# Hiding the scores that a count has found: a pass of VectorE, or four subtractions of GpSimd

## What is computed

```python
dots = einsum('bhid,bhjd->bhij', q, k) * scale          # j: 16 memory keys, then 512
dots = einsum('bhij,hk->bkij', dots, pre_proj)
dots = where(causal, -max, dots)
vk = lax.top_k(dots, 64)[0][..., -1:]                    # the 64th largest of each row
dots = where(dots < vk, -max, dots)
attn = softmax(dots)
attn = einsum('bhij,hk->bkij', attn, post_proj)
out = einsum('bhij,bhjd->bhid', attn, v) ... @ Wo + bo
```

## Time and profile before

| | |
|---|---|
| median of 3 runs | 3666.67 us |
| the profiled execution | 3667.18 us |
| its span, first to last instruction | 3665.3 us |
| granted TensorE clock, mean | 0.878 |
| busy: DVE, ACT | 3356.8 us (92%), 3202.9 us (87%) |
| busy: PE, PEld, POOL | 2800.9, 1814.3, 1432.8 us (76%, 49%, 39%) |
| DVE by line | L1017 522.2, L983 516.1, L1030 502.5, L1064 443.4, L1052 396.1 us |
| POOL by line | L1236 546.1, L1243 338.5 us |

### The profile page before, as it was taken

The page is one execution under the profiler, slowest core; times in us unless marked ns, Lnnn a source line. Parts: engine busy times, 40 slices in busy tenths (PEclk is TensorE's granted clock), DMA queues, the critical chain, the costliest instruction groups (busy, mean ns, idle before and its releaser), DMA issues. The chain is left out here.

```text
span 3665.3 us, 67866 instructions
## 1 busy us (share of the span) xinstructions
PE 2800.9 (76%) x13751; PEld 1814.3 (49%) x13751; DVE 3356.8 (92%) x13778; ACT 3202.9 (87%) x9018; POOL 1432.8 (39%) x2407
## 2 busy tenths in 40 slices
PE   7777878777767877777777767777777787777755
PEld 3455555555544555555455545554455455445544
DVE  4699999999999999999999999999999999999994
ACT  1799999999978999999999979998999999999973
POOL 3233443343334443444443334343444344343433
PEclk9888898889888989889899888989889889898986
DMA  1000000000000000000000000000000000000000
GB/s 41 7 2 2 4 8 5 8 2 5 8 4 8 5 8 2 5 8 5 8 5 8 2 4 8 5 8 2 5 8 5 8 2 6 6 5 8 2 7 4
DMA packets 31377, 22.38 MB, mean 6 GB/s; under 512 B 3202, under 2 KB 30339, under 8 KB 30723
## 3 DMA queue, kind: packets, MB, share of 16 engines
q1 hardware_dynamic: 30722, 16.03, 1.5%
HBM read 11.83 MB, written 4.19 MB: 4 GB/s over the span
## 5 line engine op out<-in xcount | busy, mean ns | idle before, releaser
L840 ACT ACTIVATE signs<-scores,state 128x528 int8<-128x528 f32 (+3 forms) x3072 | 1764.3, 574 | 200.4 <-DVE state L1122 124.0
L1236 POOL TENSOR_SCALAR probs<-probs,rinv 128x528 f32<-128x528 f32 (+3 forms) x1024 | 546.1, 552 | 1696.0 <-DVE rinv L1022 1694.8
L682 PE MATMUL s_bank<-xn,gT 128*128 128x512 f32 (+3 forms) x2048 | 916.3, 576 | 2.3 <-issue 1.5
L706 PE MATMUL t_bank<-ident,probs 128*128 128x128 f32 x2560 | 477.8, 311 | 283.5 <-POOL probs L1236 275.5
L693 PEld LDWEIGHTS y_bank<-u_all,probsT 128*128 128x128 f32 x5120 | 620.5, 195 | 134.0 <-issue 124.9
L693 PE MATMUL y_bank<-u_all,probsT 128*128 128x128 f32 x5120 | 625.3, 278 | 6.9 <-ACT probsT L851 6.8
L840 ACT ACTIVATION_READ_ACCUMULATOR signs<-scores,state 128x1 f32 x3072 | 576.0, 187 | 0.0
L1017 DVE SCALAR_TENSOR_TENSOR probs<-scores,kth,expo 128x528 f32<-128x528 f32 (+3 forms) x1024 | 522.2, 565 | 31.1 <-issue 23.6
L706 PEld LDWEIGHTS t_bank<-ident,probs 128*128 128x128 f32 x2560 | 299.1, 153 | 485.9 <-issue 380.6
L861 ACT ACTIVATE expo<-scores,negmax 128x528 f32<-128x528 f32 (+3 forms) x1024 | 535.1, 575 | 0.0
L983 DVE TENSOR_SCALAR_CACHE_REDUCE work<-scores,state 128x528 f32<-128x528 f32 (+3 forms) x1024 | 516.1, 559 | 17.8 <-issue 8.1
(11 more groups left out here) (152 smaller groups left out, 3577.7 us busy)
## 6 DMA issues: line engine op xcount, KB each, us to landing
xwork<-in_L_attn_x_dram SPq DMA_DIRECT2D x17, 256.0 KB, 2.8
xres<-in_L_attn_x_dram SPq DMA_DIRECT2D x16, 256.0 KB, 2.9
out_dram<-ybuf SPq DMA_DIRECT2D x16, 256.0 KB, 2.4
u_all<-in_L_attn_Wq_dram SPq DMA_DIRECT2D x1, 512.0 KB, 3.8
u_all<-in_L_attn_Wk_dram SPq DMA_DIRECT2D x1, 512.0 KB, 4.6
u_all<-in_L_attn_Wv_dram SPq DMA_DIRECT2D x1, 512.0 KB, 5.4
u_all<-in_L_attn_Wo_dram SPq DMA_DIRECT2D x1, 512.0 KB
expo<-in_L_ffn_w_gate_dram SPq DMA_DIRECT2D x1, 192.0 KB, 4.8
```

Of the source, the lines that this page charges most:

```text
L682: nc.tensor.matmul(score_part(t, 0, KEYS[t]), lhsT=gT[s % 2][:, t * P:(t + 1) * P], rhs=xn[par][:, 0:KEYS[t]], start=True, stop=False, ski ...
L706: mm = nc.tensor.transpose(t_bank[q % 2][:, at:at + P], probs[:, h % 2, KEY_AT[t] + j * P:KEY_AT[t] + (j + 1) * P], ident[:, :])
L840: nc.scalar.activation(signs[:, k, 0:ROW[t]], row(scores, ring(head_of(s, k + 1), RING), t), ACT.Sign, bias=state[:, s % 2, S_T, k * T + t ...
L1236: nc.gpsimd.tensor_scalar(prb, prb, rinv[:, slot_p, t:t + 1], 1.0, ALU.mult, ALU.mult).then_inc(scaled, 1)
```

## The change

L1052 goes. In its place POOL subtracts `work` from the scores, tile by tile, each as soon as DVE's count of that tile is done. So that subtracting 1 is enough to push a found score below all others, scores are kept in units of 2^60: the factor on the products that they are made of is 2^-60 smaller, the guesses, the mask and the maxima follow, and the exponential multiplies by 2^60. The counts of DVE now raise a semaphore of their own, `found_ready`, and POOL answers with `hidden`, on which MAX8 waits. On POOL the copy of the memory scores moves ahead of the subtractions, and these stand ahead of the scaling.

```diff
-MASKED = -2.0 ** 100
+UNIT = 2.0 ** -60
+MASKED = -2.0 ** 40
...
-            table[i, t] = z
-            table[i, T + t] = z - FAR / (2 * density)
+            table[i, t] = z * UNIT ** 0.5
+            table[i, T + t] = (z - FAR / (2 * density)) * UNIT ** 0.5
...
-                              DH ** -0.5).then_inc(a_taken, 1)
+                              DH ** -0.5 * UNIT).then_inc(a_taken, 1)
...
                                                  bias=negmax[:, bass.ds(ring(head_of(s, LAG_K), RING), 1), t]
+                                                 scale=1.0 / UNIT
...
 def count_found(t):
     v.tensor_scalar(work[:, AT[t]:AT[t] + ROW[t]], row(scores, slot_k, t), guessed[:, t:t + 1],
-                    None, ALU.is_ge, ALU.add, accum_out=found[:, t:t + 1]).then_inc(select_step, 1)
+                    None, ALU.is_ge, ALU.add, accum_out=found[:, t:t + 1]).then_inc(found_ready, 1)
...
-                        v.scalar_tensor_tensor(out=work[:, :], in0=work[:, :], scalar=-FMAX,
-                                               in1=scores[:, bass.ds(slot_k, 1), :].squeeze(1),
-                                               op0=ALU.mult, op1=ALU.add).then_inc(select_step, 1)
-                        dve.wait_ge(select_step, T + 2)
+                        dve.wait_ge(select_step, 2)
...
 def top_scan():
     if selects:
-        dve.wait_ge(select_step, T + 4)
+        dve.wait_ge(hidden, 4 * gk + 4)
+        alone(dve)
         for t in ORDER:
             v.max(cand[:, t, 1:9], work[:, AT[t]:AT[t] + ROW[t]]).then_inc(select_step, 1)
...
+                    if lagged(kind, s, LAG_K):
+                        slot_k = ring(head_of(s, LAG_K), RING)
+                        for p, t in enumerate(ORDER):
+                            pool.wait_ge(found_ready, 4 * (g - LAG_K) + p + 1)
+                            alone(pool)
+                            wrk = work[:, AT[t]:AT[t] + ROW[t]]
+                            nc.gpsimd.tensor_tensor(wrk, row(scores, slot_k, t), wrk, ALU.subtract).then_inc(hidden, 1)
```

More of the change, by code:

```diff
@@ L416, in build @@
         counted = [sem(f"counted{k}") for k in range(GUESSES)]
+        found_ready = sem("found_ready")
+        hidden = sem("hidden")
         select_step = sem("select_step")
@@ L935, in _ @@
             dve.wait_ge(a_taken, 4)
-            nc.vector.tensor_tensor(a_sq[:, :, :], a_all[:, :, :], a_all[:, :, :], ALU.mult).then_inc(squared, 1)
+            nc.vector.scalar_tensor_tensor(out=a_sq[:, :, :], in0=a_all[:, :, :], scalar=1.0 / UNIT, in1=a_all[:, :, :],
+                                           op0=ALU.mult, op1=ALU.mult).then_inc(squared, 1)
             dve.wait_ge(squared, 1)
@@ L1228, in step @@
                                               seed[:, s, :, :]).then_inc(first_ready, 1)
+                    if kind != "drain":
+                        if s == 0:
+                            pool.wait_ge(memmax_ready, b + 1)
+                        slot = ring(head_of(s, 0), RING)
+                        if kind != "first" or s >= RING:
+                            pool.wait_ge(probs_ready, 4 * (g - RING + 1))
+                        alone(pool)
+                        nc.gpsimd.tensor_copy(mem_parts(scores[:, bass.ds(slot, 1), :].squeeze(1)),
+                                              head_mem(smem[par], s)).then_inc(mem_placed, 1)
+                    if lagged(kind, s, LAG_K):
+                        slot_k = ring(head_of(s, LAG_K), RING)
+                        for p, t in enumerate(ORDER):
+                            pool.wait_ge(found_ready, 4 * (g - LAG_K) + p + 1)
+                            alone(pool)
+                            wrk = work[:, AT[t]:AT[t] + ROW[t]]
+                            nc.gpsimd.tensor_tensor(wrk, row(scores, slot_k, t), wrk, ALU.subtract).then_inc(hidden, 1)
                     if lagged(kind, s, LAG_P):
@@ L1243, in step @@
                         nc.gpsimd.tensor_copy(head_mem(pmem, head_of(s, LAG_P)), mem_parts(probs[:, slot_p, :])).then_inc(pmem_ready, 1)
-                    if kind != "drain":
-                        if s == 0:
-                            pool.wait_ge(memmax_ready, b + 1)
-                        slot = ring(head_of(s, 0), RING)
-                        if kind != "first" or s >= RING:
-                            pool.wait_ge(probs_ready, 4 * (g - RING + 1))
-                        alone(pool)
-                        nc.gpsimd.tensor_copy(mem_parts(scores[:, bass.ds(slot, 1), :].squeeze(1)),
-                                              head_mem(smem[par], s)).then_inc(mem_placed, 1)
                     extras(kind, b, s)
```

16 lines of the change are left out of this document (8 added, 8 removed).

## The result

The changed kernel takes 3679.9 us (median of 6 runs, 3677.9 to 3684.9) against 3667.0 us of the kernel before on the same chip: ratio 1.0037, 95% interval 1.0026 to 1.0049. It is slower, by 13 us. The forecast said slower, but by 38 us; its range, 3620 to 3850, holds the time. The profiled execution, the slowest of its six, has a span of 3683.1 us against 3665.3, 17.8 more. Its mean granted TensorE clock is 0.877 against 0.878, so the clocks are alike.

What follows compares the result with a forecast made beforehand. DVE was taken to bound the kernel, ACT close behind. Step growths of 1.05 + 0.58 + 0.15 + 0.15 + 0.45 = 2.38 us a batch made +38 us in 16 batches: 3667 + 38 = 3705 us, range 3620 to 3850.

Steps and rivals of the forecast that it cites:

- Which engine bounds: DVE, 92% busy, sets the time; ACT stands only tenths of a us behind in steps without norm or feed-forward.
- The turns: DVE instructions with two SBUF inputs, or DVE copies, alternate whole with POOL instructions reading SBUF; here masking pass and subtractions.
- the forecast order: After POOL's first subtraction, masking of 528 elements goes first, then the subtraction of 400, alternating down to 144.
- Forecast delay of the chain: Masking pass ends 1.60 us later, or 1.46 in most steps, where it already starts 0.14 later; bounds 0 and 2.67.
- the forecast's rule: The waiting engine's instruction ends 0.02 us plus its elements' time behind the other's, on DVE and on POOL.
- DVE keeps its turn: Rival: the four masking instructions run back to back, later small ones are stopped 1.3 us against 1.31 saved; 3665 us, chance 0.20.
- They do not meet: Rival: masking pass and two-input POOL instructions do not exclude each other, so 1.31 us stay saved; 3463 us, chance 0.12.
- No start-up hides: Rival: the three later subtractions cost DVE their whole time, delay 2.67 us, +1.36 a step; 4015 us, chance 0.08.
- Not the same work: Rival: counts or power on POOL fail at 1e-18, guesses miss and the full search runs; +2700 us, chance 0.02.
- The step that failed: POOL's memory-keys copy moves ahead of the subtractions, beside one-input MAX8; no cost or gain was counted for it.
- 1.31 us: Time saved per DVE step by removing L1052: 1.35 us, less 0.04 for the wait and nop ahead of MAX8.
- growth forecast: Growth by step kind: seven +0.15, two +0.29, three with f_up and three with norm +0.05, one +0.45; batch +2.38 us.

Runs made afterwards that it cites:

- the run with the fill: Changed kernel with each POOL subtraction replaced by a memset of the same tile to -1, which reads nothing: 3486.0 us, ratio 0.950.
- one input: Changed kernel with each POOL subtraction replaced by a one-input multiplication of the same tile by -1 and 1: 3484.3 us, ratio 0.950.
- the run of four elements: Changed kernel with each POOL subtraction covering only 4 elements and MAX8 reading the scores themselves: 3483.3 us, ratio 0.950.
- the run of the units alone: Changed kernel with the subtraction back on DVE as one instruction; 2^60 units, semaphores, wait and nop, and earlier memory copy stay: 3659.6 us, ratio 0.9981.
- the copy put back: Changed kernel with POOL's memory-keys copy back behind L1263, as in the kernel before; DVE's program unchanged: 3700.6 us, ratio 1.0085.
- a changed order: Changed kernel with DVE taking new scores from PSUM ahead of the masking pass, and MAX8 ahead of the small block and guess chain: 3504.3 us, ratio 0.956.

## Why the prediction was right in its mechanism and wrong in its size

**Which engine bounds.** Right. DVE sets the changed kernel; ACT waits more for turned tiles (L854 waits 210.8 us for PE, where L851 waited 109.8), and that costs DVE next to nothing, as worked out (its own wait for the counts is 20.8 us against 19.3).

**The turns.** Right. Forecast: L1022 of about 0.9, 1.4, 1.0 and 0.6 us; measured, in the 193 heads of the forecast order, 0.77 to 0.85, 1.40, 0.99 and 0.58. The forecast did not see the other order, of 51 heads; that the mean of the first, 0.94, is also close to 0.9 is luck. Forecast delay of the chain 1.46 us in steps where it starts at +2.07, and 1.60 where it starts at +1.93; measured, as medians over the batches, 1.48 and 1.57. The rule of a turn (the waiting one ends its elements plus a small constant behind the other, its start-up being over) was read from two rows, and in the 244 heads of both orders every turn ended within 0.07 us of the forecast's rule. The constant is about 0.01 us for DVE behind POOL and 0.05 for POOL behind DVE, where 0.02 was taken for both. POOL's was too small because the forecast's 1.06 ns an element compared a copy of 64 elements with a scaling of 528. The scaling's own four sizes in the run with the fill (708, 602, 499 and 390 ns) give 0.83. At that, an estimate for a copy, the one that ended 0.09 us behind L1052 had 0.05 for its elements and 0.04 besides. The Trainium skill, SBUF — State Buffer, "Who interferes with whom", says that a two-input DVE instruction contends with a GpSimd instruction that reads SBUF and not with one that only writes. The runs with one input and with the fill agree, each with its rows above. The rule of the Trainium skill against this change (Perfetto Trace Analysis, "Optimizing Scalar/DVE Operations") holds here for four tiles on POOL, and not for one (ratio 0.966).

**The rivals.** "DVE keeps its turn" wanted L1022 unchanged: it is not. "They do not meet", 3463 us, is what the run of four elements comes near to (3483): the price of not meeting was right to 20 us. "No start-up hides" wanted a delay of 2.67 us: it is 1.5. "Not the same work" fell with the run of the units alone.

**The step that failed** is a sentence that priced a moved instruction at nothing: "The copy of the memory keys (L1252) goes ahead of the subtractions, beside MAX8, which has one input." It asked what the copy meets where it goes, and not what it leaves. It leaves L1093, a two-input instruction that had waited for it in 13 of 16 steps. So the saved time is not 1.31 us. From the end of the masking chain to MAX8 it was 6.09 us in a plain step and is 4.65: 1.44 saved. With the copy put back it is 4.74, so 1.35 of this is the change without the move, close to the forecast's 1.31, and 0.09 is the move. Median steps in us of the even batches, before, with the copy put back, and after:

```
step       before    copy put back    after    growth forecast
2          12.60     12.74            12.65    +0.15
3, 5       12.52     12.66            12.57    +0.15
9, 13      12.38     12.62            12.52    +0.29
10 to 12   14.00     14.26            14.11    +0.05
6, 7       14.40     14.51            14.51    +0.05
1          12.97     13.38            13.03    +0.45
4          13.62     12.89            12.82    +0.15
14         14.77     15.29            15.31    +0.05
0, 8, 15   13.78     13.97            13.89    +0.15
all 16     215.88    218.57           217.04   +2.38
```

With the copy where it was, plain steps grow by 0.14 (forecast 0.15), steps 9 and 13 by 0.24 (0.29), step 1 by 0.41 (0.45), and the batch by 2.69 (2.57 in odd ones), against 2.38. The copy's move takes 1.5 us a batch off again (1.2 in odd ones). In timed runs that is +32 us for the change without the move, against +38 in the forecast, and -18 for the move, against nothing. That 32 lies so near to 38 is luck in part. The forecast counted sixteen equal batches, and sixteen like those measured here would make +42. The first and the last batch, the drain and the steps with a full search (0.7 to 1.4 us shorter than before) take 11 off again; why they do was not taken apart.

**Smaller terms** were off as well, and of both signs. Steps 10 to 12 grow by 0.26 with the copy put back, not by 0.05: how f_up's product meets DVE there was not taken apart. In step 4 of every second batch before has a pause of 0.88 to 1.16 us ahead of L1017, and the changed kernel has one of 0.88 to 1.11 at the same place. POOL has no such pause; its first two subtractions run from 1872.35 to 1874.64 of the trace, nearly all of it ahead of L1022's start, and the turns cost only 0.73 us. The rows of after:

```profile
1873.21 0.36 DVE L988 TENSOR_SCALAR_CACHE_REDUCE work<-scores,state 128x144 f32<-128x144 f32 x1
...
1874.45 0.77 DVE L1022 SCALAR_TENSOR_TENSOR probs<-scores,kth,expo 128x528 f32<-128x528 f32 x1 [0.88 <-issue]
1875.15 1.13 DVE L1022 SCALAR_TENSOR_TENSOR probs<-scores,kth,expo 128x400 f32<-128x400 f32 x1
1876.21 0.72 DVE L1022 SCALAR_TENSOR_TENSOR probs<-scores,kth,expo 128x272 f32<-128x272 f32 x1
1876.86 0.36 DVE L1022 SCALAR_TENSOR_TENSOR probs<-scores,kth,expo 128x144 f32<-128x144 f32 x1
```

That step becomes 0.6 to 0.9 us shorter, in every second batch. Step 14 grows by 0.5 there: a gap of 0.24 us between L1096 and L1097, in which DVE waits for nothing that the profile shows, puts later small instructions behind POOL's norm products. That reading rests on the trace alone; no run took the gap away.

## What to carry to other kernels

When two engines take turns at a memory, price every pair of instructions that the change brings together, and every pair that it parts: for each moved instruction, look at the other engine's neighbours at the old place for one that is longer than its kind. A piece of work handed to the other engine pays while it fits beside instructions that take no turns. Here 528 of 1344 elements gave 3.4%, all of them lost 0.4%, and all of them behind a changed order gave 4.4%; each of the three has the moved copy in it, which is worth 0.5% of its own.

## What the hardware showed that was not expected

- **A pause behind a branch goes by place.** One empty DVE instruction more in each step moved pauses of 1 us to other steps, and the kernel became 0.27% slower (0.17 to 0.37). That is as large as the effect that was to be explained, so a comparison within 0.3% that changes DVE's instruction count in a program with branches says little of the change itself. The Trainium skill, Runtime: NRT & Kernel Launch, "Instruction fetch mechanics", has a cause that would fit: instructions are fetched in blocks, and a taken branch to one not yet there stalls. No run here shows the fetch itself.
- **A small instruction can hide 17 us.** L1093, 12 elements a row, was 0.07 us longer on the mean than without the copy beside it (0.09 in 13 of 16 steps), and moving one 0.23 us copy on an engine that was 39% busy gave 0.46%.
- **One input takes turns, a fill does not,** on POOL's side: 843 ns and 767 ns for the same L1022.
